# Drains of TensorE's queue carry the increments of a graph attention kernel's loop

## The reference

```python
h_src = nfeats[src]
h_dst = nfeats[dst]
e = leaky_relu(concat([h_src, h_dst, efeats]) @ W_attn + b_attn, 0.01)[:, 0]
m = concat([h_src, efeats], axis=-1) @ W_ne
emax = segment_max(e, dst)
ex = exp(e - emax[dst])
alpha = ex / segment_sum(ex, dst)[dst]
z = segment_sum(alpha[:, None] * m, dst)
out = relu(concat([nfeats, z], axis=-1) @ W_out)
x = layernorm(x + out)
```

## Time and profile before

| what | value |
|---|---|
| median of 3 runs | 4999.54 us (4994.14 to 5000.15) |
| the profiled execution | 4990.13 us |
| its span, first to last instruction | 4988.3 us |
| TensorE busy, matmuls | 2010.8 us, 40% |
| VectorE busy | 2579.2 us, 52% |
| ScalarE busy | 2315.7 us, 46% |
| GpSimd busy | 2978.3 us, 60% |
| mean DMA rate | 126 GB/s |

### The profile page before, as it was taken

One profiled execution on the slowest core, in us unless ns is written; L12 is line 12 of the kernel. 1 busy time (PEld: TensorE's weight loads), 2 busy tenths in 40 slices (PEclk: granted clock), 3 DMA queues, 4 the chain that ended last, 5 costly groups with the idle time before them and its releaser, 6 DMA issues.

```text
span 4988.3 us, 64221 instructions
## 1 busy us (share of the span) xinstructions
PE 2010.8 (40%) x9870; PEld 1926.7 (39%) x9871; DVE 2579.2 (52%) x4868; ACT 2315.7 (46%) x4121; POOL 2978.3 (60%) x3149
## 2 busy tenths in 40 slices
PE   1444444434343334443434333434333433343346
PEld 0334444433333333333433333433333333343346
DVE  5555455555554555555555555545555555555556
ACT  1455555444444444444444444444444444444444
POOL 6566666666666666666666666656666666666651
PEclk9666666666666666666666666666666666666666
DMA  5444444444444444444444444444444444454441
GB/s 111 122 130 126 128 129 132 128 129 129 127 127 128 130 129 130 130 127 124 131 128 127 127 130 130 130 129 128 126 129 127 129 129 130 123 136 128 126 129 53
DMA packets 759570, 628.92 MB, mean 126 GB/s; under 512 B 608412, under 2 KB 608796, under 8 KB 759332
## 3 DMA queue, kind: packets, MB, share of 16 engines
q1 hardware_dynamic: 646164, 519.51, 36.2%
q0 software_dynamic: 100096, 102.60, 11.1%
q10 hardware_dynamic: 13072, 4.80, 0.5%
HBM read 621.58 MB, written 4.81 MB: 126 GB/s over the span
## 4 chain that ended last, share of the span: by engine, by line
issue 31%; another core or an unknown queue 17%; ACT 17%; DVE 15%; DVEq 10%; ACTq 7%; PE 1%; POOL 0%
ACT zb L508 4%; ACT psE L507 4%; DVE prod L619 3%; DVE u L623 3%; DVEq L741 2%; ACTq L513 2%; ACT acc L471 2%; DVE um L728 2%; ACT pT L461 2%; DVE acc L682 2%; ACT psS L499 2%; DVE e L689 1%; DVEq L708 1%; ACT ebias L502 1%
## 5 line engine op out<-in xcount | busy, mean ns | idle before, releaser
L365 POOL DMA_INDIRECT V<-in_x_dram,srcs x3128 | 2953.4, 944 | 1883.4 <-PEq L892 951.2
L851 PE MATMUL psT<-ident,e 128*128 128x128 f32 x3136 | 757.9, 421 | 2593.2 <-ACT pT L461 1249.6
L851 PEld LDWEIGHTS psT<-ident,e 128*128 128x128 f32 x3136 | 615.5, 219 | 2664.2 <-issue 2399.5
L857 PE MATMUL psG<-V,pT 128*128 x6288 | 1237.3, 379 | 13.4 <-DVE acc L682 11.2
L857 PEld LDWEIGHTS psG<-V,pT 128*128 128x128 f32 x6288 | 1232.3, 299 | 15.3 <-issue 15.2
L461 ACT COPY pT<-psT 128x512 f32<-128x512 f32 x784 | 434.0, 579 | 1348.6 <-remote 1301.4
L619 DVE TENSOR_TENSOR prod<-V,psM 128x1024 f32<-128x1024 f32 x391 | 477.6, 1221 | 828.0 <-issue 827.9
L728 DVE CUSTOM_DVE_ANT_0 um<-ubc,psS 128x1024 f32<-128x1024 f32 x391 | 476.5, 1219 | 617.1 <-issue 315.6
L623 DVE TENSOR_REDUCE u<-prod 128x8 f32<-128x1024 f32 x391 | 477.0, 1220 | 62.5 <-issue 22.4
L689 DVE TENSOR_TENSOR e<-zb,psE 128x1024 f32<-128x1024 f32 x392 | 475.5, 1213 | 10.6 <-issue 8.0
L499 ACT ACTIVATE psS<-dbc,nbias 128x1024 f32<-128x1024 int32 x391 | 437.0, 1118 | 12.8
(11 more groups left out here) (95 smaller groups left out, 656.3 us busy)
## 6 DMA issues: line engine op xcount, KB each, us to landing
ubc<-scores SPq DMA_DIRECT2D x391, 512.0 KB
dbc<-in_dst_dram SPq DMA_DIRECT2D x390, 512.0 KB
V<-in_edge_attr_dram SPq DMA_DIRECT2D x390, 256.0 KB
V<-in_x_dram,srcs POOLq DMA_INDIRECT x3128
scores<-u SPq DMA_DIRECT2D x391, 4.0 KB
srcs<-in_src_dram SPq DMA_DIRECT2D x390, 4.0 KB
out_dram<-y SPq DMA_DIRECT2D x12, 256.0 KB
xt<-in_x_dram ACTq DMA_DIRECT2D x6, 448.0 KB
```

Source lines behind the costliest of these rows:

```text
L365: nc.gpsimd.indirect_dma_start(V[0:n, s, j, 0:F], None, x[:, :], bass.IndirectOffsetOnAxis(ap=srcs[0:n, s, j:j + 1], axis=0)).then_inc(h_i ...
L851: last = nc.tensor.transpose(psT[:, i, j * P:(j + 1) * P], e1[:, :].rearrange("q (p j) -> q j p", j=J)[:, 4 * i + j, :], ident[:, :])
L857: last = nc.tensor.matmul(psG[:, 0:AW], pT[:, i, j * P:(j + 1) * P], V[:, bass.ds(sv, 1), 4 * i + j, :].rearrange("p a f -> p (a f)"), sta ...
```

## The change

The increments leave TensorE's matmuls in the loop, and five drains of its queue carry them:

```diff
@@ y_pair
-                y_multiply().then_inc(y_ready, 1)
+                y_multiply()
+                pe.drain().then_inc(y_ready, 1)
@@ turn(i)
-                last.then_inc(tr[i], 1)
@@ multiply(i, sv)
-                last.then_inc((agg_half, agg_done)[i], 1)
@@ window(turns)
                     turn(0)
                     turn(1)
+                    pe.drain().then_inc(tr[0], 1)
+                    pe.drain().then_inc(tr[1], 1)
                 pe.wait_ge(merged, G + 1)
                 multiply(0, sv)
                 multiply(1, sv)
+                pe.drain().then_inc(agg_half, 1)
+                pe.drain().then_inc(agg_done, 1)
@@ supertile(t, s, ahead)
                     pe.load(coming, trip[0:1, bass.ds(2 * t + 3, 1)])
-                    pe.wait_ge(agg_done, pe.snap(g))
-                    pe.sem_inc(v_free[(s - BEHIND) % RING], 1)
+                    pe.drain().then_inc(v_free[(s - BEHIND) % RING], 1)
```

More of the change, by code:

```diff
@@ L850, in turn @@
                 for j in range(4):
-                    last = nc.tensor.transpose(psT[:, i, j * P:(j + 1) * P], e1[:, :].rearrange("q (p j) -> q j p", j=J)[:, 4 * i + j, :], ident[:, :])
-                last.then_inc(tr[i], 1)
+                    nc.tensor.transpose(psT[:, i, j * P:(j + 1) * P], e1[:, :].rearrange("q (p j) -> q j p", j=J)[:, 4 * i + j, :], ident[:, :])
             def multiply(i, sv):
                 for j in range(4):
-                    last = nc.tensor.matmul(psG[:, 0:AW], pT[:, i, j * P:(j + 1) * P],
-                                            V[:, bass.ds(sv, 1), 4 * i + j, :].rearrange("p a f -> p (a f)"),
-                                            start=(i == 0 and j == 0), stop=(i == 1 and j == 3))
-                last.then_inc((agg_half, agg_done)[i], 1)
+                    nc.tensor.matmul(psG[:, 0:AW], pT[:, i, j * P:(j + 1) * P],
+                                     V[:, bass.ds(sv, 1), 4 * i + j, :].rearrange("p a f -> p (a f)"),
+                                     start=(i == 0 and j == 0), stop=(i == 1 and j == 3))
             def window(turns):
```

## The result

The changed kernel takes 5515.64 us (median of 4 runs, 5464.35 to 5550.24) against 4996.84 us of the kernel before, run beside it (4993.93 to 5000.15): a ratio of 1.1004, 95% interval 1.0929 to 1.1078. The ratio is that of the means, without the one run of 5550.24 us, which was over 1.5% above the fastest; the medians as they stand give 1.1038. The profiled execution took 5464.35 us, its span is 5462.5 us, 474 us more than the 4988.3 before.

The account below looks back on a forecast made before the run. TensorE's completions, late while gathers run, were taken to hold up the ring. 1.1 us in each of 313 waiting bursts, 344 us, on the 4988.3 us span gave 5332, with run overheads 5345 us; range 4560 to 5620.

Parts of the forecast that it names:

- The sign and the mechanism: Whole kernel: slower, chance 0.60; TensorE's completions arrive late while gathers run, and the ring waits for them.
- The choice on which all rested: TensorE's drains beside gathers: a drain is held as the increments are; forecast 5345 us, chance 0.37.
- v_free behind the products' drain: TensorE's sequencer work and drains behind the products: v_free 1.1 us later in each of 313 waiting bursts, 344 us.
- The transposes' drains: Two drains between TensorE's transposes and products: bounds nothing to some 0.5 us, taken as 0.
- they wait for merged anyway: TensorE's products behind the transposes' drains: they wait for merged in any case, so the drains' lower bound is nothing.
- the products' end is followed by idle time and not the reverse: TensorE in the loop: idle time follows the products, so the transposes' drains ahead of them were taken as 0.
- its upper bound: If transposes' drains are held too, products start late: up to 3.6 us in 77 bursts, 277 us more, 5620.
- The y pairs' drains: Drain behind the y product on TensorE, 50 in all, 0.1 us each: 5 us at most, left out.
- Rival 1: TensorE's drains are not held and the ring runs free: faster, 4600 us, chance 0.26.
- both met every time: GpSimd's 10.0 us pace and the compute chain's 8.2 plus 1.1 us, met in every tile: 4060 us.
- Rival 2: Drains not held, GpSimd never pauses, the other sequencers crawl: slower, 5450 us, chance 0.21.
- Rival 3: A wash: the late v_free is hidden, or a gain and the 1.1 us cancel: 5000 us, chance 0.08.

Follow-up runs that it names:

- the kernel without a drain: Kernel before plus one more TensorE wait for agg_done right behind the products, all increments kept: 4023.09 us (0.9999) and 4025.14 us (1.0005), both in free series.
- the release three tiles back: Kernel before with BEHIND = 3, v_free released behind the completion of one window earlier, no drain: 4024.89 us (1.0000), free series.

## Why the prediction was right or wrong

**The sign and the mechanism were right.** The choice on which all rested, that a drain is held as an increment is, is what the trace shows: L876 takes 6.8 us in the middle. A copy of L461 that waited starts 2.9 us after the start of the latest gather in the kernel before and 2.8 us in the changed one (medians, 342 each): the increment and the drain let it go at the same point of the burst. After the last gather the way from the products to the copy is short: products at 5329.44, 2.94 us long, and the copy starts at 5332.49.

```profile
5329.44 2.94 PE L857 MATMUL psG<-V,pT 128*128 x16 [0.47 <-issue]
...
5332.49 1.07 ACT L461 COPY pT<-psT 128x512 f32<-128x512 f32 x2
```

"PSUM — Partial Sum Buffer" of the Trainium skill (section "Engine vs sequencer instructions") says that a drain waits until the engine is fully idle. The trace agrees in that no drain ended before the work ahead of it; but in held series it ends up to 12 us after the last matmul's modelled end (2497.37 to 2508.85 above), so in such a tile "idle" is told late.

**The sum was right in part by luck.** It gave +344 us (its terms add up to 5344, the text has 5345), and +519 was measured (5515.64 − 4996.84). Its two terms fared thus:

*v_free behind the products' drain.* Taken as 1.1 us × 313 bursts = 344. The 1.1 us is what the traces show (0.80 to 1.75 us is 0.95, 0.80 to 1.89 is 1.09). In it, the sequencer's 0.9 us were right, and the drains nearly: they take 8 to 13 ns, but the second follows the first by 0.10 us. In the tile above L894's drain ends 1.05 us after L876's. The count was wrong. Alone this part costs 206 us: with it 117 bursts adjoin for 66 before, and only 237 wait for the increment. A later release doesn't delay every burst: bursts that found their slot free are 117 + 35 for 66 + 18 (pauses under 2 us), as if a late burst lets the other engines catch up for the next; that reading is argued, the counts are shown.

*The transposes' drains.* Taken as 0, and mis-sized the most: alone they cost 402 us. The step that failed is "they wait for merged anyway", and "the products' end is followed by idle time and not the reverse". Both hold at a burst that began behind a pause of over 2 us, which is most of them. In 84 tiles, 83 of them at a burst that adjoined or nearly adjoined the one before, the drain stands for the burst, mostly until 3 to 4.3 us after its last gather's start. In the kernel before such a tile had one hold for transposes and products together: in the earlier trace rows the products were done at 2503.79, and the copy came at 2511.71, 4.3 us after the start of the burst's last gather (2507.40). In the tile above the transposes' drain ends 4.3 us after such a start as well, and only then the products begin. Gather to gather, the burst of the earlier trace rows paused 2512.62 − 2507.40 − 1.25 = 3.97 us, the one above 2514.96 − 2504.57 − 1.25 = 9.14. The 5.2 us between them are 0.44 from drain to products, 3.9 for the products and 0.84 from copy to gather. The text had this as its upper bound, 3.6 us × 77 = 277 us on top. Its count was good: 77 bursts that didn't wait, 77 pauses of over 6 us, of which 62 came next behind an adjoining burst. Before, the pause behind such a burst was one of 3 to 4.2 us (55 of 65). Its price held neither the way from the drain to the products nor the copies that come behind them.

*Together.* 206 + 402 is 608 us, and the change costs 517 to 519. The parts overlap, and with both there are fewer long drains (84 and 97 in the two runs, for 150). Why was not tested. The two parts also come from two series, whose kernels before differ by 47 us (4935.29 and 4981.93).

**Checks that the text had set.** The mean wait of the gathers was to rise from 3.0 to 4.1 us and became 5.06; the period was to be 13.4 us and is 13.6 (mean between starts of L728); TensorE's gap between transposes and products was to stay under 0.6 us: it is 0.46 us on the mean in 308 windows and 10.3 in the other 85, 1014.3 us in all, by the recorded starts of the matmuls. That check names the failed step exactly. In the kernel before the same sum is 13.4 us. The y pairs' drains are too few to be seen: 49 in the trace (the text has 50), 0.88 us in the middle, 5.5 at most.

**Rival 1** (not held, the ring runs free) is no effect of the change, but it is what a free series is, before and with each part of the change: 4024 us, where the text had 4060 for "both met every time". It would need completions to come in time, and the change doesn't bring that about. **Rival 2** (adjoining bursts make the other sequencers crawl) is half right. VectorE's branch L708 in the kernel before, held, and in the free series in the kernel with the transposes' drains alone, where all bursts but one adjoin:

```profile
L708 DVEq COMPARE_BRANCH  x391: 5/49/840, 87.6 to 4896.5; - x196
...
L708 DVEq COMPARE_BRANCH  x391: 43/49/67, 67.1 to 3929.2; - x196
```

In the free series it is never above 67 ns. So adjoining bursts alone don't make it. But in the held series the crawl goes with them: instructions of VectorE's sequencer at 640 to 900 ns are 584 before, 617 after, 919 with the transposes' drains alone and 1072 with the products', at 66, 78, 106 and 117 adjoining bursts, 8 to 9 for each; 476 of the 584 and 529 of the 617 began while such a burst ran. What the crawl itself costs no run shows. That the change makes bursts adjoin more often, and that the next pause is then a long one, is the part of this rival that came true; its condition, drains that are not held, did not. **Rival 3** named a real thing, that a late release is partly made good, at 138 of 344 us, and not at all of it. "TensorE: Matmul & The Clock Gate" of the Trainium skill (section "The cost: per-tile semaphore tail") gives 26 ns for each increment, 41 us for the four of a window, an estimate from that page. The free series can't show it, since the gathers set the time there; with four gathers, where they don't, the change costs 122 us all the same.

**Left open.** What makes a series held or free, and what it is in a burst that holds TensorE's completions: the traces show the when, not the cause. That the held transposes lie at adjoining bursts is a count and was not tested by a run either. And, as said, whether the 1.1 us is the sequencer's work alone; the copy-to-gather times say so, no held run of the kernel without a drain does. The drain of v_free alone and the release three tiles back met only free series as well.

## What to carry to other kernels

A drain carries what the last instruction's increment would have carried, and adds an order: all that is queued behind it waits for the completion of all ahead of it. Before putting one in, list what follows on that queue and needs nothing of what came before; here this was the products of another window, and alone it cost 402 us, for 206 of the rest. And read how late completions come beside other engines' work before counting on an instruction's nominal end: here it was microseconds late beside bursts of eight gathers.

## What the hardware showed

- Beside a burst of 8 indirect gathers (10 us) TensorE's completions came late in held series, increments and drains alike: up to 12 us for transposes, ending mostly 3 to 4.3 us after the start of the burst's last gather, and with the change 83 of 84 times at bursts that followed the one before within 2 us. With bursts of 4 gathers, in the same series as a held kernel, the transposes' drain took 1.95 us at most and the products' 2.6 us in the middle.
- The kernel before took 4024 to 4025 us or 4935 to 4997 us, within a series stable to 0.3%, and one chip gave a time of either kind in two series. In a free series no more than 2 instructions of VectorE's sequencer took 640 to 900 ns, for 584 in the held kernel before, and all bursts but one adjoined. Gather for gather GpSimd was as fast in both (944 ns and 0.30 us between two).
- A drain of TensorE took 8 to 13 ns on an idle engine, and put 0.43 to 0.47 us between the last matmul's modelled end and the next matmul's start, which had come 0.2 us ahead of that end without it.
- The change costs 10% in held series; each of its three parts costs 0.0% in a free one. The whole of it was measured in held series alone.
